# A transformer layer on one core: other buffers and another order in the opening, a division and a count moved

## The chip, the cores and the metric

The kernel runs on one core of one Trainium2 chip. The metric is the device time of one execution in microseconds; lower is better. Engines are called by their names and by their letters in the profile: TensorE (PE, and PEld for its weight loads), VectorE (DVE), ScalarE (ACT), GpSimd (POOL), SyncE (SP, which only issues DMAs).

## The reference

Eight sequences of 512 tokens with 256 channels go through attention, a layer norm, a mixture of experts with a shared expert, and a second layer norm. Cut to what matters:

```python
qkv = x @ w_qkv.T                       # 16 heads of 16 channels
q, k = rms_norm(q, q_norm_w), rms_norm(k, k_norm_w)
q, k = rope(q, k, cos, sin)             # q1*cos - q2*sin, q2*cos + q1*sin
attn = softmax(causal(q @ k.T) * scale)
x = layernorm(x + (attn @ v) @ w_proj.T)
normed = x * rsqrt(mean(x*x) + 1e-8) * norm_weight
shared = relu(normed @ sw1 + sb1) @ sw2 + sb2
probs = sigmoid(normed @ router_w.T); scores, idx = top_k(probs, 2)
routed = sum over the 2 chosen experts of weight * (relu(normed @ ew1 + eb1) @ ew2 + eb2)
x = layernorm(x + shared + routed)
```

## The kernel before

All matrix products run in fp16 on TensorE with each fp32 operand split in a high and a low half, so that one product is three (high by high, high by low, low by high).

**Steps.** The front (0 to 465 us) works on the eight batches (sequences) in an order written out by hand. Every engine runs through the same numbered steps, g from -40 to 209, and in each step does what is due in it, in the order in which its `step` function lists the kinds of work. An engine's queue is strictly in order. A table such as `QK = (-28, -24, -20, -16)` gives the step of each of the four token tiles, counted from 20 times the batch's number; for batches 0 and 1 the table `OPENING` gives other steps. Twenty units of scores (`UNITS`) of batch c stand in steps 20c to 20c + 19, so the steps below 0 are the opening, in which only batch 0 is prepared.

**What prepares a tile n (four a batch).** TensorE makes its q and k (`QK`) into a PSUM bank. ScalarE copies them (`copied`, L861) and squares them (L864). GpSimd multiplies the swapped halves by the sines (`swap`, two products, L667 and L670) into `rsum`. VectorE multiplies by the cosines (`rope`, L1111, into `rot`), sums the squares (L1118), and adds both (`summed`, L1126). For each pair of tiles ScalarE takes the inverse root (`roots`, step `ROOT`) and VectorE refines it in three small steps (`refined`, L1134 to L1136, step `REFINE`). VectorE scales (`normed`, L1141, step `QN`) into `qn`. GpSimd casts that to the high half (`nat_high`, L679), VectorE makes the low half (`nat_low`, L1151), and GpSimd doubles both for stacked contractions (`nat_twice`, L686 and L687). TensorE turns q and k (`stacked`, L1598 and L1604, step `TR`) through the banks `ma` and `mc`, and they are copied into `stk` by ScalarE (L950, L955) and VectorE (L1377). The unit 0 of a batch waits until all four tiles are in `stk`. The buffers `rsum`, `qn` and `nat` hold two tiles each. The bank `ma` is used in turn by the QK products from batch 1 on, the turned q and the V products, and each user waits for the copy of the one before it.

**Attention and after.** `scores` (L1553, L1562) fill two slots in turn; ScalarE takes the exp (`exps`, L847); `attended` multiplies by V (L1575). The rows are turned back (`NAT`, L1710) through the one bank `mb`; VectorE divides them by their sums (`averaged`, L1159 and L1160), which frees `mb` for the next tile. Then come the projection, the layer norm (GpSimd's `norms` and `shifted`), VectorE's normalised rows (`normalised`, L1200 to L1204), the turned normalised rows (`XN`, L1613, copied by ScalarE in L977), the router's product (`LG`, L1734), the choice of two experts (`chosen`, ending in the mask of L1224), the ranks (`RANK`), and GpSimd's scatter of the rows to the experts' regions (L717).

**The early tiles.** From step 161 on, the shared expert's first six tiles of 256 tokens run beside the last batches: H pieces are half of a hidden product (L1641, 24 matmuls), O pieces half of an output product (L1678). ScalarE takes the relu of an H piece (`early_hidden`, L902) and its high half (L906) one step later, and VectorE the low half (`early_low`, L1332) three steps later. Relus wait for the low half of the piece that used their buffer before.

**The tables.** In step `TABLE` (197) TensorE adds up how many rows each expert got (`counted`, L1622), once the last batch's ranks are summed; VectorE then works out the tables of tiles (`tables`), which the routed part (from 465 us on, L1786 and L1802) reads.

The changed functions are printed here with the line numbers of the profile.

Of the kernel before, what the change touches and what calls it, by code (L numbers as in the profile page):

```python
# [7 lines left out]
ALU = mybir.AluOpType  # L8
# [60 lines left out]
def wait_apart(eng, S, name, count):  # L69
# [10 lines left out]
MORE_WEIGHTS = -29  # L80
# [33 lines left out]
    QK: ((-40, -39, -38, -37), (0, 1, 3, 5)),  # L114
    ROPE: ((-40, -39, -36, -35), (1, 2, 4, 6)),
    ROOT: ((-38, -34), (2, 7)),
    REFINE: ((-37, -33), (4, 8)),
    QN: ((-37, -36, -33, -32), (4, 5, 8, 10)),
    V: ((-36, 2), (8, 22)),
    SPLIT_X: ((None,), (-31,)),  # L120
    TR: ((-28, -27, -26, -25), (9, 11, 14, 18)),
# [50 lines left out]
assert len(EARLY_AT) == 4 * N_EARLY and list(EARLY_AT) == sorted(EARLY_AT) and N_EARLY % 2 == 0  # L172

# [66 lines left out]
def program(nc, a, S, keep):  # L240
# [87 lines left out]
    with ExitStack() as ctx:  # L328
# [117 lines left out]
        with nc.Block() as block:  # L446
# [176 lines left out]
            def _(pool):  # L623
# [33 lines left out]
                def swap(n):  # L657
# [8 lines left out]
                    r1 = rsum[:, n % 2, :].rearrange("p (k h d) -> p k h d", k=2, d=HD)  # L666
# [7 lines left out]
                def nat_high(n):  # L674

                    pool.wait_ge(S("qn_done"), n + 1)
                    if n >= 2:
                        pool.wait_ge(S("tk_done"), n - 1)
# [3 lines left out]
                def nat_twice(n):  # L682

                    pool.wait_ge(S("nat_lo"), n + 1)
                    q, k = nat[:, n % 2, 0], nat[:, n % 2, 1]
# [126 lines left out]
            def _(act):  # L812
# [52 lines left out]

                def roots(c, u):
# [51 lines left out]
                def early_step(g):  # L918
# [6 lines left out]
                    for kind, m, q in early_due(g - 1):  # L925
# [15 lines left out]
                def step(g):  # L941
# [6 lines left out]
                    for c, t in due(TR, g):  # L948
# [4 lines left out]
                        if c == 0 and t < NT - 1:  # L953
# [104 lines left out]
            def _(dve):  # L1058
# [62 lines left out]
                def summed(c, t):  # L1121
# [4 lines left out]
                    then(dve.tensor_tensor(rsum[:, n % 2, :], rot[:], rsum[:, n % 2, :], ALU.add), "rsum_done", n + 1)  # L1126
# [11 lines left out]
                def normed(c, t):  # L1138
# [3 lines left out]
                                           rsum[:, n % 2, :].rearrange("p (h d) -> p h d", d=HD),  # L1142
# [3 lines left out]
                def nat_low(c, t):  # L1146
# [3 lines left out]
                    half = nat[:, n % 2].rearrange("p k h d -> p (k h) d")  # L1150
# [206 lines left out]
                def step(g):  # L1357
# [13 lines left out]
                    for c, t in due(TR, g):  # L1371
                        if c == 0 and t < NT - 1:
# [7 lines left out]
                    for c, t in due(NAT, g):  # L1380
                        averaged(c, t)
# [147 lines left out]
            def _(pe):  # L1529
# [62 lines left out]
                def stacked(c, t):  # L1592
# [4 lines left out]
                    for i in range(8):  # L1597
                        last = pe.transpose(ma[:, 64 * i:64 * i + 64].bitcast(F16),  # L1598
                                            nat[:, n % 2, 0, 2 * i:2 * i + 2, :].rearrange("p h d -> p (h d)"), ident_h[:])
# [324 lines left out]
```

## Time and profile before

| | |
|---|---|
| median of 3 runs | 982.53 us (982.53 to 987.88) |
| the profiled execution | 980.02 us, span 978.3 us |
| TensorE busy | 906.0 us (93%) |
| VectorE busy | 606.2 us (62%) |
| ScalarE busy | 626.0 us (64%) |
| GpSimd busy | 475.5 us (49%) |
| mean granted TensorE clock | 0.981 |

The span is the time from the first to the last instruction of the one execution that was profiled; all rows are from it. Busy times are summed over the instructions of an engine. Matmuls are pipelined and overlap a little in the records, so sums of their times are a few per cent high. The granted clock is 1.00 for TensorE's full 2.4 GHz and 0.50 for its half.

### The profile page before, as it was taken

The numbers are of one execution on the slowest core, as the hardware profiler recorded it, in microseconds if no ns is written. First come the engines' busy times: TensorE is split into PE (matmuls) and PEld (weight loads), VectorE is DVE, ScalarE is ACT, GpSimd is POOL, SyncE is SP. The second block draws the span as 40 slices with busy tenths as digits, with TensorE's granted clock in tenths as the row PEclk, the third lists the DMA queues.
The fourth block names the chain that finished last, engine by engine and source line by source line (L and its number), as shares of the span: only waits on it lengthen the run. The fifth ranks groups of instructions, "written<-read, shape, count | busy, mean of one in ns | idle before, by whom it ended". The sixth has DMA issues, their size and how long they took to land.

```text
span 978.3 us, 26286 instructions
## 1 busy us (share of the span) xinstructions
PE 906.0 (93%) x9049; PEld 694.1 (71%) x9050; DVE 606.2 (62%) x1197; ACT 626.0 (64%) x1027; POOL 475.5 (49%) x664
## 2 busy tenths in 40 slices
PE   3689899898999898989999999999999999999995
PEld 1344555454555546878989888998899988688885
DVE  7676799889898955875334444454433332327975
ACT  3688898787888776634655565556544544456753
POOL 5574566877777655474234454344434444312311
PEclk9699999999999999999999999999999999999998
DMA  5112223434323255587872121121212111139751
GB/s 171 66 66 91 93 98 105 136 108 154 110 88 115 104 171 184 192 287 260 283 249 65 49 70 57 63 65 54 70 50 65 55 61 62 46 102 287 224 162 44
DMA packets 69811, 116.98 MB, mean 120 GB/s; under 512 B 7808, under 2 KB 46080, under 8 KB 69600
## 3 DMA queue, kind: packets, MB, share of 16 engines
q1 hardware_dynamic: 52352, 81.51, 25.2%
q10 hardware_dynamic: 10896, 16.40, 5.8%
q0 software_dynamic: 6480, 17.97, 5.0%
q8 instruction: 51, 0.84, 0.3%
q14 instruction: 32, 0.26, 0.1%
HBM read 68.67 MB, written 47.18 MB: 118 GB/s over the span
## 4 chain that ended last, share of the span: by engine, by line
PE 65%; POOL 12%; DVE 9%; issue 6%; ACT 6%; DMA 1%; ACTq 0%; POOLq 0%; DVEq 0%; SPq 0%
PE yb L1802 25%; PE hb L1786 25%; PE pv_bank L1575 3%; PE yb L1678 2%; ACT prob L847 2%; POOL xg_rows L717 2%; PE hb L1641 2%; PE ma L1588 2%; POOL nat L679 2%; PE tr L1661 2%; POOL nat L686 1%; PE slot L1553 1%; POOL rsum L667 1%; POOL rsum L670 1%; POOL vv L696 1%
## 5 line engine op out<-in xcount | busy, mean ns | idle before, releaser
L1011 ACT ACTIVATE hf<-hb,b 128x256 f32<-128x256 f32 (+1 forms) x392 | 155.5, 454 | 212.8 <-PE hb L1786 193.8
L1786 PE MATMUL hb<-xgT,wts 128*128 128x256 f16 (+1 forms) x1872 | 219.0, 263 | 2.7 <-ACT hf L1011 2.7
L1802 PE MATMUL yb<-wts,hh 128*128 x1704 | 215.3, 273 | 0.0
L1430 DVE TENSOR_TENSOR hh<-hf,hh 128x1024 f16<-128x1024 f32 (+1 forms) x98 | 118.4, 1212 | 149.8 <-ACT hh L1016 149.8
L1786 PEld LDWEIGHTS hb<-xgT,wts 128*128 x1872 | 177.8, 98 | 25.4 <-issue 4.3
L782 POOL DMA_INDIRECT y_tok<-yb,dest x71 | 77.1, 1085 | 235.4 <-DVE yb L1442 225.2
L847 ACT ACTIVATE prob<-slot 128x1024 f32<-128x1024 f32 x160 | 162.3, 1044 | 32.4 <-PE slot L1562 32.1
L1802 PEld LDWEIGHTS yb<-wts,hh 128*128 128x128 f16 x1704 | 166.4, 98 | 21.2
L1016 ACT ACTIVATE hh<-hf 128x1024 f16<-128x1024 f32 (+1 forms) x98 | 97.6, 996 | 3.1
L717 POOL DMA_INDIRECT xg_rows<-xnh,sl_i x64 | 73.7, 1152 | 16.2 <-issue 13.9
L1442 DVE SCALAR_TENSOR_TENSOR yb<-yb,b2bc 128x512 f32<-128x512 f32 (+1 forms) x39 | 25.1, 643 | 86.7 <-PE yb L1802 81.6
L1553 PE MATMUL slot<-stk 64*128 64x128 f16 (+3 forms) x512 | 64.1, 309 | 15.5 <-ACT prob L847 8.9
L1575 PE MATMUL pv_bank<-prob,vst 128*32 128x512 f32 (+3 forms) x1024 | 75.5, 436 | 1.1 <-ACT prob L847 1.1
L1588 PE MATMUL ma<-wqkv,xTh 128*128 128x256 f16 (+1 forms) x360 | 67.6, 333 | 4.1 <-ACT raw L864 2.2
L1575 PEld LDWEIGHTS pv_bank<-prob,vst 128*32 128x32 f32 x1024 | 30.0, 109 | 44.9 <-issue 37.6
L1562 PE MATMUL slot<-mask_b,ident_b 128*128 128x256 bf16 (+1 forms) x320 | 57.2, 262 | 0.0
L1786 PE MATMUL hb<-xgT,wts_s 128*128 128x256 f16 x480 | 54.0, 273 | 0.0
L1802 PE MATMUL yb<-wts_s,hh 128*128 128x256 f16 x480 | 53.9, 273 | 0.0
L1588 PEld LDWEIGHTS ma<-wqkv,xTh 128*128 128x128 f16 x360 | 34.8, 102 | 24.2 <-issue 5.1
L1802 PEld LDWEIGHTS yb<-wts_s,hh 128*128 128x128 f16 x480 | 47.0, 98 | 5.4
L1786 PEld LDWEIGHTS hb<-xgT,wts_s 128*128 128x128 f16 x480 | 47.0, 98 | 5.4
L1553 PEld LDWEIGHTS slot<-stk 64*128 64x128 f16 x512 | 17.2, 94 | 45.6 <-issue 18.2
(217 smaller groups left out, 1483.2 us busy)
## 6 DMA issues: line engine op xcount, KB each, us to landing
wts<-in_w_all SPq DMA_DIRECT2D x19, 512.0 KB, 4.9
stage<-in_w_all SPq DMA_DIRECT2D x16, 512.0 KB, 4.5
w_split<-chunk_hl SPq DMA_DIRECT2D x16, 512.0 KB, 3.0
wts<-y_tok SPq DMA_DIRECT2D x32, 256.0 KB, 4.8
xg<-xg_rows ACTq DMA_DIRECT2D x30, 264.0 KB, 2.7
wts<-w_split SPq DMA_DIRECT2D x3, 2048.0 KB, 9.8
xTf<-in_xT SPq DMA_DIRECT2D x8, 512.0 KB, 4.1
xin<-in_x SPq DMA_DIRECT2D x8, 512.0 KB, 4.2
```

The costliest lines, as they stand in the source:

```text
L717: pool.indirect_dma_start(a["xg_rows"], bass.IndirectOffsetOnAxis(ap=sl_i[:, c % 2, t, k:k + 1], axis=0), xnh[:, c % 2, t, :], None).then_ ...
L782: pool.indirect_dma_start(a["y_tok"], bass.IndirectOffsetOnAxis(ap=dest[:, slot, j:j + 1], axis=0), yb[:, par, j, :], None).then_inc(S(f"y ...
L847: act.activation(dst, src, ACT.Exp, scale=ATT_SCALE).then_inc(S("exp_done"), 1)
L1011: act.activation(hf[:, c, 0:size], hb[c // 2][:, (c % 2) * TT:(c % 2) * TT + size], ACT.Relu, bias=bias, scale=1.0 / WS).then_inc(S("relu_ ...
L1016: act.activation(hh[:, par, 0, cs, 0:size], hf[:, cs, 0:size], ACT.Copy).then_inc(S("h_hi"), 1)
L1430: dve.tensor_tensor(hh[:, par, 1, cs, 0:size], hf[:, cs, 0:size], hh[:, par, 0, cs, 0:size], ALU.subtract).then_inc(S("h_lo"), 1)
L1553: pe.matmul(slot[:, 512 * x + col:512 * x + col + T - P * j], stk[rows, par, 1, pr, P * j:P * j + P], stk[rows, par, 0, pr, P * j:T], star ...
L1562: last = pe.matmul(out, ident_b[:], mask_b[:, 0:diag[0], :], start=False, stop=True, skip_group_check=True)
L1575: last = pe.matmul(pv_bank[32 * r:32 * r + 32, P * j:T], vst[:, c % 2, j, 4 * g + r, :], prob[:, g % 2, r, SEG[j]:SEG[j] + T - P * j], sta ...
L1588: last = pe.matmul(out, xTh[:, c % 2, x, k, P * t:P * t + P], wqkv[:, y, k, cols], start=(n == 0), stop=(n == len(pieces) - 1))
L1786: ins = pe.matmul(hb[hc // 2][:, (hc % 2) * TT:(hc % 2) * TT + size], weights(e, c, w, hc * P, P), xgT[:, par, x * DC + c, 0:size], start= ...
L1802: ins = pe.matmul(ybank[par][:, j * D:(j + 1) * D], hh[:, par, x, hc, P * j:P * j + P], weights(e, DC + hc * D // CH, w, hc * D % CH, D), ...
```

## The change

Four parts.

1. **The opening.** The high halves of batch 0's four tiles go from GpSimd to ScalarE (`first_high`). Tiles 2 and 3 of batch 0 get halves and sums of their own, in the part of `prob` that is not in use yet (`halves`, `rotated`), so that they wait neither for `qn` nor for the turned rows. Tile 0 is turned in step -33; the turned k of tiles 1 and 2 is now copied by VectorE, like that of tile 3 before. The next x^T is split, and the projection's weights too, some steps later.
2. **Batch 1's order.** Its first two QK products stand in steps -2 and -1, ahead of unit 0, and use the banks `mb` and `pv_bank`; their halves and turns come sooner; its V product goes from step 8 to 13.
3. **The first division sooner.** For tile 0 of every batch `averaged` moves from the head of step NAT to the tail of the step before it on VectorE, ahead of the normalised rows of the batch before.
4. **The end of the front.** ScalarE's relus of the piece ("H", 3, 1) come three steps later, in step 189, so that the last turned normalised rows (step 188) are copied ahead of them. TensorE's `counted` stands behind the early piece of its step instead of ahead of it.

The diff, cut to its core:

```diff
-MORE_WEIGHTS = -29
+MORE_WEIGHTS = -24
...
 OPENING = {
-    QK: ((-40, -39, -38, -37), (0, 1, 3, 5)),
-    ROPE: ((-40, -39, -36, -35), (1, 2, 4, 6)),
-    ROOT: ((-38, -34), (2, 7)),
-    REFINE: ((-37, -33), (4, 8)),
-    QN: ((-37, -36, -33, -32), (4, 5, 8, 10)),
-    V: ((-36, 2), (8, 22)),
-    SPLIT_X: ((None,), (-31,)),
-    TR: ((-28, -27, -26, -25), (9, 11, 14, 18)),
+    QK: ((-40, -39, -38, -37), (-2, -1, 3, 5)),
+    ROPE: ((-40, -39, -36, -35), (-1, 0, 4, 6)),
+    ROOT: ((-38, -34), (1, 7)),
+    REFINE: ((-37, -33), (2, 8)),
+    QN: ((-37, -36, -33, -32), (2, 4, 8, 10)),
+    V: ((-35, 2), (13, 22)),
+    SPLIT_X: ((None,), (-28,)),
+    TR: ((-33, -28, -27, -26), (7, 10, 14, 18)),
 }
...
+def early_relu_due(g):
+
+    return [piece for at, piece in EARLY if at + (4 if piece == ("H", 3, 1) else 1) == g]
...
-            return ma[:, 0:2 * D]
+            return (mb, pv_bank, ma, ma)[t][:, 0:2 * D] if c == 1 else ma[:, 0:2 * D]
+
+        def halves(n):
+
+            if n in (2, 3):
+                return prob[:, 1, n - 2, 0:1024].bitcast(F16).rearrange("p (k h d) -> p k h d", k=2, h=NH)
+            return nat[:, n % 2]
+
+        def rotated(n):
+
+            return prob[:, 1, n, 0:2 * D] if n in (2, 3) else rsum[:, n % 2, :]
...
                     pool.wait_ge(S("qk_copied"), n + 1)
-                    if n >= 2:
+                    if n >= NT:
                         pool.wait_ge(S("qn_done"), n - 1)
...
                     for c, t in due(QN, g - 1):
-                        nat_high(4 * c + t)
+                        if c >= 1:
+                            nat_high(4 * c + t)
...
+                def first_high(n):
+
+                    act.wait_ge(S("qn_done"), n + 1)
+                    act.activation(halves(n)[:, :, :, 0:HD].rearrange("p k h d -> p (k h) d"),
+                                   qn[:, n % 2, :].rearrange("p (h d) -> p h d", d=HD), ACT.Copy).then_inc(S("nat_hi"), 1)
...
-                    for kind, m, q in early_due(g - 1):
+                    for kind, m, q in early_relu_due(g):
                         if kind == "H":
                             early_hidden(m, q)
...
-                        if c == 0 and t < NT - 1:
+                        if c == 0 and t == 0:
                             act.wait_ge(S("tk_done"), t + 1)
                             act.activation(stk[:, 0, 1, :, t * P:(t + 1) * P],
...
+                    for c, t in due(QN, g - 1):
+                        if c == 0:
+                            first_high(t)
                     for c, u in due(ROOT, g):
                         roots(c, u)
...
                     for c, t in due(TR, g):
-                        if c == 0 and t < NT - 1:
+                        if c == 0 and t == 0:
                             continue
...
                     for c, t in due(NAT, g):
-                        averaged(c, t)
+                        if t > 0:
+                            averaged(c, t)
...
                     for c, t in due(ROPE, g):
                         rope(c, t)
+                    for c, t in due(NAT, g + 1):
+                        if t == 0:
+                            averaged(c, t)
                     for c, u in rows_due(g):
                         normalised(c, u)
...
                         if c >= 1:
                             pe.wait_ge(S("xT_lo"), c + NT)
-                            pe.wait_ge(S("ma_free"), NTH["qk", c, t])
+                            if c >= 2 or t >= 2:
+                                pe.wait_ge(S("ma_free"), NTH["qk", c, t])
...
-                    if g == TABLE:
-                        counted()
                     for kind, m, q in early_due(g):
...
                             if m == N_EARLY - 1 and q == 1:
                                 turn_rows(0, 1)
+                    if g == TABLE:
+                        counted()
```

## Rows read from the trace of the kernel before

**Rows 1.** Windows view: busy us of PE, PEld, DVE, ACT, POOL; then clock, DMA.
```profile
500.00:978.00 478.00, 465.51 (x4472) 413.21 (x4470) 229.10 (x352) 263.59 (x502) 170.49 (x245) 0.99 0.29 91
```

**Rows 2.** Chain of waits, 165 to 260 us, its share by line.
```profile
by line: issue 22.3%; POOL xg_rows L717 14.2%; POOL rsum L667 5.4%; POOL vv L696 5.4%; POOL nat L679 5.2%; POOL nat L686 4.9%; POOL rsum L670 4.2%; POOL vv L706 3.6%; POOL y L745 3.6%; POOL nat L687 2.9%; DVE nat L1151 2.1%; POOL vv L704 2.
```

**Rows 3.** GpSimd's timeline, opening: start, us, line, operation, idle before.
```profile
14.56 1.17 POOL L670 TENSOR_TENSOR rsum<-raw,stab 128x256 f32<-128x256 f32 x1
...
18.34 1.13 POOL L679 CAST nat<-qn 128x512 f16<-128x512 f32 x1 [2.62 <-DVE qn L1141]
...
30.61 0.61 POOL L679 CAST nat<-qn 128x512 f16<-128x512 f32 x1 [0.80 <-PE mc L1604]
...
34.28 1.07 POOL L687 COPY nat<-nat 128x512 f16<-128x512 f16 x1
```

**Rows 4.** VectorE's timeline, opening.
```profile
16.80 0.23 DVE L1134 TENSOR_TENSOR nt<-ry 128x64 f32<-128x64 f32 x1 [0.28 <-ACT ry L876]
...
17.58 1.42 DVE L1141 TENSOR_TENSOR qn<-rsum,rn 128x512 f32<-128x512 f32 x2
...
26.80 0.52 DVE L1135 SCALAR_TENSOR_TENSOR nt<-ms,nt 128x64 f32<-128x64 f32 x1
...
32.35 1.51 DVE L1410 TENSOR_TENSOR xTh<-xTf,xTh 128x1024 f16<-128x1024 f32 x1
```

**Rows 5.** ScalarE's timeline, 19 to 49 us.
```profile
19.25 0.60 ACT L966 ACTIVATE vst<-ma 128x512 f32<-128x512 f32 x1 [1.57 <-PE ma L1588]
...
39.15 1.02 ACT L847 ACTIVATE prob<-slot 128x1024 f32<-128x1024 f32 x1 [1.64 <-PE slot L1562]
...
48.61 1.02 ACT L847 ACTIVATE prob<-slot 128x1024 f32<-128x1024 f32 x1
```

**Rows 6.** TensorE's timeline, 38 to 62 us.
```profile
38.17 0.61 PE L1553 MATMUL slot<-stk 64*128 64x512 f16 x2 [0.88 <-DVE stk L1377]
...
38.90 2.77 PE L1588 MATMUL ma<-wqkv,xTh 128*128 128x512 f16 x6
...
48.85 1.46 PE L1588 MATMUL ma<-wqkv,xTh 128*128 128x512 f16 x6 [0.85 <-ACT vst L966]
...
61.60 0.61 PE L1598 MATMUL ma<-keep_ident,nat 128*128 128x128 f16 x8 [2.48 <-ACT vst L966]
```

**Rows 7.** Windows view as above, around unit 0 and after the count.
```profile
38.00:44.00 6.00, 5.64 (x20) 1.83 (x21) 1.31 (x3) 3.13 (x4) 1.62 (x2) 0.54 0.50 197
...
436.00:440.00 4.00, 4.00 (x25) 2.88 (x22) 3.54 (x23) 0.84 (x2) 2.44 (x3) 0.57 1.02 382
```

**Rows 8.** Who waited for whom on TensorE, 100 to 375 us.
```profile
PE mb L1710 <- DVE an L1160: 9.1, 5, 2.5
```

**Rows 9.** VectorE's timeline, one batch of the middle.
```profile
223.08 2.55 DVE L1200 SCALAR_TENSOR_TENSOR xnf<-y,vv,ffn_nw 128x256 f32<-128x256 f32 x2
```

**Rows 10.** TensorE's timeline, 430 to 448 us.
```profile
430.16 0.95 PE L1734 MATMUL mc<-wrout,xnT 128*128 128x8 f16 x32 [2.24 <-ACT xnT L977]
...
435.77 0.26 PE L1622 MATMUL mc<-keep_msum,ones_h 128*128 128x8 f16 x4 [1.83 <-DVE keep_msum L1243]
...
435.89 7.07 PE L1641 MATMUL hb<-xgT,wts_s 128*128 128x256 f16 x48
...
442.79 5.40 PE L1678 MATMUL yb<-wts_s,hh 128*128 128x256 f16 x48
```

**Rows 11.** ScalarE's timeline, 429 us.
```profile
429.10 1.01 ACT L977 ACTIVATE xnT<-mc 128x1024 f16<-128x1024 f16 x1
```

**Rows 12.** VectorE's timeline, 429 to 450 us.
```profile
429.22 2.23 DVE L1332 TENSOR_TENSOR hh<-hf,hh 128x1024 f16<-128x1024 f32 x1 [2.60 <-ACT hh L906]
...
433.07 0.19 DVE L1224 TENSOR_TENSOR mh<-oh 128x32 f16<-128x32 f32 x1
...
447.54 2.34 DVE L1332 TENSOR_TENSOR hh<-hf,hh 128x1024 f16<-128x1024 f32 x2
```

**Rows 13.** GpSimd's timeline, 429 us.
```profile
429.11 1.26 POOL L769 TENSOR_TENSOR rs<-rs,b2s 128x512 f32<-128x512 f32 x1 [0.39 <-DMA rs<-resid]
```

More of the change, by code:

```diff
@@ L662, in swap @@
                     pool.wait_ge(S("qk_copied"), n + 1)
-                    if n >= 2:
+                    if n >= NT:
                         pool.wait_ge(S("qn_done"), n - 1)
                     q4 = qk_copy(n).rearrange("p (k h d) -> p k h d", k=2, d=HD)
-                    r1 = rsum[:, n % 2, :].rearrange("p (k h d) -> p k h d", k=2, d=HD)
+                    r1 = rotated(n).rearrange("p (k h d) -> p k h d", k=2, d=HD)
                     pool.tensor_tensor(r1[:, :, :, 0:hd2], q4[:, :, :, hd2:HD],
@@ L676, in nat_high @@
                     pool.wait_ge(S("qn_done"), n + 1)
-                    if n >= 2:
-                        pool.wait_ge(S("tk_done"), n - 1)
+                    pool.wait_ge(S("tk_done"), n - 1)
                     pool.tensor_copy(nat[:, n % 2, :, :, 0:HD].rearrange("p k h d -> p (k h) d"),
@@ L684, in nat_twice @@
                     pool.wait_ge(S("nat_lo"), n + 1)
-                    q, k = nat[:, n % 2, 0], nat[:, n % 2, 1]
+                    q, k = halves(n)[:, 0], halves(n)[:, 1]
                     pool.tensor_copy(q[:, :, 2 * HD:4 * HD], q[:, :, 0:2 * HD]).then_inc(S("nat_ready"), 1)
@@ L1125, in summed @@
                     dve.wait_ge(S("swap_done"), 2 * (n + 1))
-                    then(dve.tensor_tensor(rsum[:, n % 2, :], rot[:], rsum[:, n % 2, :], ALU.add), "rsum_done", n + 1)
+                    then(dve.tensor_tensor(rotated(n), rot[:], rotated(n), ALU.add), "rsum_done", n + 1)
                 def refined(c, u):
@@ L1141, in normed @@
                     then(dve.tensor_tensor(qn[:, n % 2, :].rearrange("p (h d) -> p h d", d=HD),
-                                           rsum[:, n % 2, :].rearrange("p (h d) -> p h d", d=HD),
+                                           rotated(n).rearrange("p (h d) -> p h d", d=HD),
                                            rn[:, t, :].unsqueeze(2).broadcast_to([P, 2 * NH, HD]), ALU.mult),
@@ L1149, in nat_low @@
                     dve.wait_ge(S("nat_hi"), n + 1)
-                    half = nat[:, n % 2].rearrange("p k h d -> p (k h) d")
+                    half = halves(n).rearrange("p k h d -> p (k h) d")
                     then(dve.tensor_tensor(half[:, :, HD:2 * HD], qn[:, n % 2, :].rearrange("p (h d) -> p h d", d=HD),
@@ L1598, in stacked @@
                         last = pe.transpose(ma[:, 64 * i:64 * i + 64].bitcast(F16),
-                                            nat[:, n % 2, 0, 2 * i:2 * i + 2, :].rearrange("p h d -> p (h d)"), ident_h[:])
+                                            halves(n)[:, 0, 2 * i:2 * i + 2, :].rearrange("p h d -> p (h d)"), ident_h[:])
                     last.then_inc(S("tq_done"), 1)
@@ L1604, in stacked @@
                         last = pe.transpose(mc[:, 64 * i:64 * i + 64].bitcast(F16),
-                                            nat[:, n % 2, 1, 2 * i:2 * i + 2, :].rearrange("p h d -> p (h d)"), ident_h[:])
+                                            halves(n)[:, 1, 2 * i:2 * i + 2, :].rearrange("p h d -> p (h d)"), ident_h[:])
                     last.then_inc(S("tk_done"), 1)
```

## The prediction

> **What bounds the kernel now.** Read first how little of the time the change can touch: from the last early tile on, TensorE is busy 465.5 of 478 us at full clock [rows 1], so that part only moves to the left by what is saved ahead of it. The change lives in the front, 0 to 465 us, and there three regimes follow one another in the chain of waits. In the opening (11 to 38 us) the chain runs through GpSimd's and VectorE's small steps while TensorE mostly waits. From 45 to 120 us it runs through TensorE and ScalarE. From 120 to 325 us it hardly leaves GpSimd and VectorE: table scatters, swaps, norms, halves [rows 2]. The reader should see that a wait of TensorE removed in the third regime is not a gain by itself.
>
> **The opening's limit is a shared resource.** A GpSimd copy of 512 elements takes 0.61 us alone and 1.13 when VectorE is in a two-input step [rows 3]; a small two-input step of VectorE takes 0.23 alone and 0.52 behind GpSimd [rows 4]. Start and end times fit strict turns: each waits until the other's instruction has ended. I therefore count turns: 0.60 for a large two-input step of VectorE and for a GpSimd product, 0.53 for a GpSimd copy, 0.2 for a small step.
> The Trainium skill (SBUF — State Buffer, the shared port pair) states an exclusive lock between GpSimd and a VectorE instruction with two SBUF inputs, in which the loser fully blocks; by this rule the trace agrees. If instead they only slowed each other evenly, the same sum would come out, so it changes no term.
>
> **Part 1, opening.** Removed from GpSimd: four high halves, 4 x 0.53 = 2.1 us of turns, now on ScalarE at 0.60 each (the V copy of the same 512 fp32 elements [rows 5]), where it waits anyway. Moved behind the fourth pair of turned rows: the low half of the next x^T, 1.1 of its 1.51 us [rows 4], and the low parts of the projection weights, 0.7. Removed waits: swaps 2 and 3 no longer wait for a buffer, since halves and sums of tiles 2 and 3 have their own.
> Step by step: GpSimd's second swap ends at 15.73 [rows 3], as before. Swap 2 now starts at once and takes turns with the sum and the three refining steps, which before began at 16.80 and took 0.23 each with GpSimd silent [rows 4]. Swaps 2 and 3 are four turns of 0.60 from 15.7; the sum ends at 17.0, refining at 19.2 instead of 17.55. So the first part gets **1.6 us later**: qn 0 and 1 at 19.9 and 20.6 (before, 1.42 from 17.58 [rows 4]). Now it pays back: product, row sums and low half of tile 2 and 0 until 22.5; GpSimd doubles tile 0 at 24.8; sum, product, sums, low half of the others until 25.5; tile 1 doubled at 27.4; refining 27.9; qn 2 and 3 at 28.6 and 29.3; low halves 30.0 and 30.7 with no wait for GpSimd's half and none for the turned rows (before 0.80 [rows 3]); tiles 2 and 3 doubled at 31.8 and 32.9. Before, the last doubling ended at 35.35 [rows 3]: **2.4 us sooner**. The bounds: if every turn falls badly 34.3, if none does 31.4.
> Then TensorE. Turned tile 3: ScalarE's copy of tile 2 ends about 33.9, transposes to 35.8 at the low clock. The x^T half, queued on VectorE behind tile 2's copy, lands at 35.2 and is covered by them. Now both products of batch 1 stand **ahead of** unit 0: 35.9 to 38.5, and 41.0 if the clock stays low (the first took 2.77 [rows 6]), 40.6 or less if it rises. Unit 0 moves from 38.17 [rows 6] to 41.1, the first exp from 39.15 to about 42.0. But the products no longer stand between the units: from 42.0 the exps run nearly back to back, exp 3 starts at 46.2 (before 48.61 [rows 5]) and batch 1's third product at 46.3 instead of 48.85 [rows 6]. **Term 1: -2.6 us** (bounds -1.1 and -4.5: the bounds of the doubling, and a rise of the clock in the middle of the products, worth 0.9 at most here: 6 matmuls take 2.77 at 0.54 and 1.46 later [rows 6, 7]).
>
> **Part 2, batch 1's order.** The V product leaves step 8, where the turn behind it waited 2.48 us for its copy at the end of ScalarE's queue [rows 6]. Turns now stand at 7 and 10, V at 13 between a QK product (12) and a turn (14): two trips to ScalarE and back there, which I cost at 0.5 us for the copy and the square behind one exp, as after 48.85. ScalarE stayed busy through most of the 2.48, so not all of it is worth anything: **Term 2: -1.0** (0 to -2.0). The first products of batch 1 in mb and pv_bank free ma and cost nothing; their readers are done before pv is written.
>
> **Part 3, first division sooner.** In batches 2 to 5 TensorE stood five times, 9.1 us in all, until VectorE had divided tile 0 of the attended rows, which was queued behind the normalised rows [rows 8]; of these the two scalings alone take 2.55, since scatters hold them up [rows 9]. Now the division comes first. It adds a wait: normalised rows, and GpSimd's and TensorE's use of them four steps later, stand behind the transposes of the next step. In the batches with a backlog these are done already. What is late next: VectorE has the same list of work, so the second division comes when it came, and TensorE stops there, about 2.5 us further on. As the chain in this regime is GpSimd's and VectorE's [rows 2], little reaches the end. **Term 3: -1.0** (0 to -9.1).
>
> **Part 4, the count behind the product.** TensorE stood 1.83 us for the last batch's sums [rows 10], and so late that the 48 matmuls behind them took 7.07 against 5.40 at full clock [rows 10], with 0.57 granted [rows 7]. Now H40 goes at once. The rows' copy, at 429.10 behind four relus [rows 11], now goes ahead of them, which takes away the 2.24 at the router product [rows 10]. But this does not arrive. The choice of experts on VectorE stands behind the low half of H31. That now starts some 0.9 (the copy) after 429.22, but it ran 2.23 only because GpSimd held the turn to 430.37 [rows 12, 13]; it still ends at 431.4, so the mask is ready at 433.26 as before [rows 12]. The idle time merely moves ahead of the ranks: H40 starts at 433.7 instead of 435.89. **Term 4: -2.2.** Counting comes at 436.4, by when VectorE has made the tables' constants; the tables delay the low half of H40, which ended 448.7 [rows 12]; its user O40 comes at 449.5 without a stop. Bounds -1.2 (the stop is 1 us) and -2.2.
> **Term 5, clock there:** 7.07 - 5.40 = 1.67 if it does not fall, 0 if it does behind the new 2 us of idle time; I take **-0.7**.
>
> **Sum:** 2.6 + 1.0 + 1.0 + 2.2 + 0.7 = 7.5 us. The profiled execution took 980.02 (span 978.3), so 972.5 by it; the median of the runs, 982.53, is 2.5 above it, and the runs spread by 5.3. I forecast for the median: 982.5 - 7.5 = **975.0**.
>
> **Rivals.** (a) *TensorE's waits for the division are real time.* Then term 3 is -9.1 and the clock stays up in those batches: 975.0 - 8.1 = 966.9. For it: ScalarE idled behind these waits too. Against it: the chain. 0.15. (b) *Only the tail works.* Collisions of swaps and refining cost what the halves give, and the new wait for V at 13 replaces the old: terms 1 to 3 are 0, 982.5 - 2.9 = 979.6. 0.25. (c) *Slower: the softmax starts too late.* Unit 0 behind two products at the low clock; with the doubling at its upper bound the first exp starts at 43.4, 4.3 later than 39.15. If ScalarE's exps pace the next 80 us, the delay stays; less 2.2 of the tail and 0 elsewhere, 982.5 + 2.1 = 984.6. It decides when TensorE and ScalarE are without gaps between exp 0 and exp 3; before, exp 3 came 9.5 after exp 0 [rows 5], which four exps of 1.02 leave mostly open, so I give it 0.07. (d) *The count gives nothing*, since the early tiles wait for the tables instead: 975.0 + 2.9 = 977.9. 0.08. My forecast: 0.45.
>
> **How the numbers follow.** The forecast's own range by its bounds is 970 to 979. To hold 8 in 10 I take 967 to 981. About 1% (9.8 us) is what a measurement here tells from no change. Faster by more than that, under 972.7: all of (a) and a quarter of the forecast, 0.27. Slower by over 1%, above 992.4: no case reaches it, 0.02. Within: 0.71.
>
> **What would show it.** GpSimd's last doubling at 32.9 and no row of L679's kind before 40; refining near 18 to 19 with 0.5 each; exp 0 near 42 but exp 3 near 46; no 2.48 at the first turn of batch 1; in batches 2 to 5 a wait for the second division where there was one for the first, and VectorE's and GpSimd's chain as long as before; H40 about 6.8 us ahead of 435.9, with about 2 us of idle time ahead of the ranks. Wrong would make it: products at a low clock beyond 41, a QK product waiting for x^T, or batches of the middle whose length changes by more than 1 us.

## The result and the profile after

The changed kernel takes **977.73 us** (median of 9 runs, 974.94 to 982.55) against 984.62 for the kernel before beside it (9 runs, 982.53 to 990.1): ratio **0.9927, interval 0.9910 to 0.9945**, some 7.2 us faster. Measured again beside the last experiments it was 975.36 against 980.56, ratio 0.9948 (0.9934 to 0.9963), 5.2 us by the medians. The forecast was 7.5. The profiled execution took 976.9 us (span 975.2; before 980.02 and 978.3), with a mean clock of 0.981, as before. So the two profiles that are compared below differ by 3.1 us only, less than half of the timed gain: the execution of the kernel before that was profiled was faster than each of its nine timed runs.

From the last early tile on nothing changed but the place: 462.43 of 475 us busy at the same clock, as in [rows 1].

```profile
500.00:975.00 475.00, 462.43 (x4444) 410.40 (x4440) 228.03 (x351) 262.75 (x501) 168.80 (x245) 0.99 0.29 91
```

**The opening.** First VectorE's timeline, which answers to [rows 4], then GpSimd's, to [rows 3] (start, us, line, operation, idle before).

```profile
16.51 0.63 DVE L1158 TENSOR_TENSOR nt<-ry 128x64 f32<-128x64 f32 x1
```

```profile
31.33 0.61 POOL L701 COPY prob<-prob 128x512 f16<-128x512 f16 x1
```

The refining steps are nearly three times as long (0.63 to 0.65 against 0.23), since GpSimd's second pair of swaps now runs beside them. This repays itself: the last doubling ends at 31.94 instead of 35.35. TensorE's timeline answers to [rows 6].

```profile
34.78 2.23 PE L1616 MATMUL mb<-wqkv,xTh 128*128 128x512 f16 x6
36.85 1.46 PE L1616 MATMUL pv_bank<-wqkv,xTh 128*128 128x512 f16 x6
38.24 0.39 PE L1581 MATMUL slot<-stk 64*128 64x512 f16 x2
...
45.09 1.46 PE L1616 MATMUL ma<-wqkv,xTh 128*128 128x512 f16 x6 [1.95 <-ACT vst L990]
...
57.93 0.61 PE L1581 MATMUL slot<-stk 64*128 64x512 f16 x2 [2.99 <-ACT prob L862]
```

Both products stand ahead of unit 0, which starts where it started before (38.24 against 38.17). How long the first of them takes differs from one execution to the next, with the clock: 1.47 to 2.71 us in the five profiles with parts 1 and 2, and unit 0 starts at 37.18 to 39.02 in them. Batch 1's third product is 3.76 us sooner. But a new stop of 2.99 us stands at 57.93, and in the windows view the clock (the third figure from the end) is at its low level from 57 to 64 us, 0.53, where it was at the high one before. First the kernel before, then the changed one:

```profile
57.00:64.00 7.00, 4.52 (x50) 2.81 (x51) 6.79 (x10) 6.81 (x11) 5.65 (x6) 1.00 0.40 140
57.00:64.00 7.00, 6.07 (x42) 2.92 (x46) 4.19 (x7) 4.75 (x5) 3.70 (x4) 0.53 0.65 225
```

ScalarE's timeline shows what TensorE waits for. Between two exps stand the copy of the turned q of batch 1's first tile, three steps of the root and the high half of x^T, 2.7 us from the first to the next exp:

```profile
53.71 0.59 ACT L867 ACTIVATE raw<-pv_bank 128x512 f32<-128x512 f32 x1
54.19 1.03 ACT L971 ACTIVATE stk<-ma 128x1024 f16<-128x1024 f16 x1
55.09 0.36 ACT L892 ACTIVATE ms<-ssq,eps 128x64 f32<-128x64 f32 x1
...
55.93 1.04 ACT L1012 ACTIVATE xTh<-xTf 128x1024 f16<-128x1024 f32 x1
56.87 3.05 ACT L862 ACTIVATE prob<-slot 128x1024 f32<-128x1024 f32 x3
```

**The middle.** Who waited for whom on TensorE, 100 to 375 us; the first row answers to [rows 8].

```profile
PE mb L1739 <- DVE an L1184: 10.0, 6, 3.5
PE slot L1581 <- ACT prob L862: 6.4, 11, 1.2
```

The wait for the division has not become smaller, 10.0 us against 9.1 (9.7 to 10.2 in the five profiles with the division sooner and the rows in their old place, 9.0 to 11.9 in the five with neither moved); it is now the second division that TensorE waits for. Yet batches 2 to 5 are shorter, by 0.78, 0.62, 1.32 and 0.63 us, measured from one second division to the next.

**The end of the front.** TensorE's timeline answers to [rows 10].

```profile
425.67 0.94 PE L1763 MATMUL mc<-wrout,xnT 128*128 128x8 f16 x32
426.47 2.78 PE L1706 MATMUL yb<-wts_s,hh 128*128 128x256 f16 x24
431.24 0.19 PE L1770 MATMUL mc<-mh,tri_h 128*128 128x32 f16 x1 [1.99 <-DVE mh L1248]
...
431.46 4.45 PE L1669 MATMUL hb<-xgT,wts_s 128*128 128x256 f16 x24
...
435.84 2.78 PE L1669 MATMUL hb<-xgT,wts_s 128*128 128x256 f16 x24
```

The idle time ahead of the router's product is gone and stands, 1.99 us of it, ahead of the ranks. The first 24 matmuls of the early product run at the low clock (4.45 against the 2.78 of the next 24), as they did in the kernel before. VectorE's timeline says why the ranks are no sooner than the batch itself: the choice begins behind the early low half, 2.08 us sooner than before (431.37), which is all the lead that the front had at that place.

```profile
428.02 1.34 DVE L1356 TENSOR_TENSOR hh<-hf,hh 128x1024 f16<-128x1024 f32 x1 [3.49 <-ACT hh L927]
429.29 0.18 DVE L1234 TENSOR_SCALAR lg<-mc 128x32 f32<-128x32 f32 x1
```

### The profile page after: what moved, and what is told of

It reads as the page before. It is cut to its first block, busy times and chain, and to the rows that moved or that the text cites. A ratio compares the mean times of both kernels' runs of the same rounds, so it can differ in the third digit from the quotient of the medians.

```text
span 975.2 us, 26284 instructions
## 1 busy us (share of the span) xinstructions
PE 906.3 (93%) x9049; PEld 695.5 (71%) x9050; DVE 601.4 (62%) x1199; ACT 626.9 (64%) x1029; POOL 466.4 (48%) x660
## 4 chain that ended last, share of the span: by engine, by line
PE 66%; POOL 10%; DVE 9%; ACT 7%; issue 6%; DMA 0%; ACTq 0%; POOLq 0%; DVEq 0%; SPq 0%
PE hb L1815 25%; PE yb L1831 24%; PE pv_bank L1603 4%; PE yb L1706 3%; ACT prob L862 2%; PE hb L1669 2%; POOL xg_rows L731 2%; PE slot L1581 2%; PE tr L1689 2%; PE ma L1616 1%; PE slot L1590 1%; POOL nat L693 1%; POOL rsum L682 1%; POOL y L759 1%; POOL vv L710 1%
## 5 line engine op out<-in xcount | busy, mean ns | idle before, releaser
L731 POOL DMA_INDIRECT xg_rows<-xnh,sl_i x64 | 76.1, 1189 | 16.2 <-issue 13.9
L1616 PE MATMUL ma<-wqkv,xTh 128*128 128x256 f16 (+1 forms) x348 | 61.6, 321 | 5.1 <-ACT raw L879 2.1
L810 POOL TENSOR_TENSOR rstd_f<-var_eps,keep_mhalf 128x2 f32<-128x2 f32 x16 | 11.9, 743 | 77.0 <-DVE var_eps L1521 77.0
```

Of the source, the lines that this page charges most:

```text
L731: pool.indirect_dma_start(a["xg_rows"], bass.IndirectOffsetOnAxis(ap=sl_i[:, c % 2, t, k:k + 1], axis=0), xnh[:, c % 2, t, :], None).then_ ...
L1616: last = pe.matmul(out, xTh[:, c % 2, x, k, P * t:P * t + P], wqkv[:, y, k, cols], start=(n == 0), stop=(n == len(pieces) - 1))
```

## The experiments

Ratios are to the kernel before on the same chip, with a 95% interval. The first four kernels shared one set of runs of before (median 985.81 us), the next four another (981.66), the last four a third (980.56). A gain in us is the ratio's share of that median, where it doesn't say "by the medians"; the two ways differ by up to 0.7 us.

**Parts 1 and 2 alone.** The changed kernel with parts 3 and 4 undone (the edit is cut):

```diff
-    return [piece for at, piece in EARLY if at + (4 if piece == ("H", 3, 1) else 1) == g]
+    return [piece for at, piece in EARLY if at + 1 == g]
...
                     for c, t in due(NAT, g):
-                        if t > 0:
-                            averaged(c, t)
+                        averaged(c, t)
...
-                    for c, t in due(NAT, g + 1):
-                        if t == 0:
-                            averaged(c, t)
...
+                    if g == TABLE:
+                        counted()
                     for kind, m, q in early_due(g):
```

> Parts 1 and 2 alone (opening and batch 1's order); the first division and the end of the front are as in the kernel before. My theory: the third QK product of batch 1 starts 3 to 4 us before 48.85, as in the trace of the changed kernel (45.09), but the turn of batch 1's tile 0, now in step 7, gathers four other tasks of ScalarE between two exps, so some 3 us are given back by 60 us, and the whole is 0 to 3 us faster than before. Rival 1 (the prediction's sum, terms 1 and 2): 3.6 us faster, kept to the end. Rival 2 (only the tail works): no difference.

Measured: 983.0 us, ratio 0.9978 (0.9961 to 0.9995), 2.2 us. That is within the expected 0 to 3; the prediction's 3.6 for the two parts lies just inside the interval (0.5 to 3.8 us).

**Part 3 alone**, in the kernel before:

```diff
                     for c, t in due(NAT, g):
-                        averaged(c, t)
+                        if t > 0:
+                            averaged(c, t)
...
                         rope(c, t)
+                    for c, t in due(NAT, g + 1):
+                        if t == 0:
+                            averaged(c, t)
```

> Part 3 alone: the first division moved ahead of the normalised rows, all else as before. The prediction: 1.0 us faster, as TensorE's wait for the first division becomes one for the second. Rival (a): 8 to 9 us faster. Middle theory from the trace of the changed kernel, where each of batches 2 to 5 is shorter by 0.6 to 1.3 us: 3 to 4 us faster by the start of batch 5's divisions.

Measured: 981.71 us, ratio 0.9962 (0.9942 to 0.9981), 3.7 us, as the middle theory had it; neither the prediction's 1.0 nor rival (a)'s 8 to 9 lies in the interval (1.9 to 5.7 us).

**Part 4 alone**, in the kernel before:

```diff
+    return [piece for at, piece in EARLY if at + (4 if piece == ("H", 3, 1) else 1) == g]
...
-                    for kind, m, q in early_due(g - 1):
+                    for kind, m, q in early_relu_due(g):
...
-                    if g == TABLE:
-                        counted()
                     for kind, m, q in early_due(g):
...
+                    if g == TABLE:
+                        counted()
```

> Part 4 alone: relus of one piece behind the last turned rows' copy, count behind H40. The prediction: 2.2 us faster at H40 counted from the choice of experts, and the same 2.2 at the first routed tile. Rival from the trace of the changed kernel: 2.2 at H40, but only 1.0 at the first routed tile, as the clock was low under H40 and H50 stopped for a while.

Measured: 983.57 us, ratio 0.9982 (0.9967 to 0.9998), 1.8 us. The interval (0.2 to 3.3 us) holds the prediction's 2.2 and the rival's 1.0.

**Part 1 alone.** As parts 1 and 2 alone, with batch 1's order and banks put back:

```diff
-    QK: ((-40, -39, -38, -37), (-2, -1, 3, 5)),
+    QK: ((-40, -39, -38, -37), (0, 1, 3, 5)),
...
-    V: ((-35, 2), (13, 22)),
+    V: ((-35, 2), (8, 22)),
...
-    TR: ((-33, -28, -27, -26), (7, 10, 14, 18)),
+    TR: ((-33, -28, -27, -26), (9, 11, 14, 18)),
...
-            return (mb, pv_bank, ma, ma)[t][:, 0:2 * D] if c == 1 else ma[:, 0:2 * D]
+            return ma[:, 0:2 * D]
```

> Part 1 alone: halves on ScalarE and own buffers in the opening, batch 1's order as before, its products behind units 0 and 1 in bank ma. My theory: unit 0 of batch 0 starts about 3 us sooner than 38.17, all of that is kept to 60 us, and the kernel is 2 to 4 us faster than before and at least as fast as with both parts. Rival: batch 1's order is what pays, then this one is within 1 us of before.

Measured: 982.73 us, ratio 0.9973 (0.9956 to 0.9989), 2.7 us, within the expected 2 to 4.

**What the four tell.** 2.2 + 3.7 + 1.8 = 7.7 us for the parts against 7.2 for the whole: they add up, as far as intervals of 1.5 to 2 us to either side of each part can tell. Part 1 alone gives as much as parts 1 and 2. The division, timed so, gives two to nearly six times what I had given it. In the trace of part 1 alone TensorE's timeline shows unit 0 at 35.76, 2.4 us sooner than before, of the 3.5 by which the last doubling is sooner there (it ends at 31.84 instead of 35.35):

```profile
35.76 0.61 PE L1577 MATMUL slot<-stk 64*128 64x512 f16 x2 [0.88 <-DVE stk L1401]
...
58.60 0.61 PE L1622 MATMUL ma<-keep_ident,nat 128*128 128x128 f16 x8 [2.24 <-ACT vst L990]
```

The old stop at batch 1's first turn is there too (2.24; 2.48 in [rows 6]). So part 2 exchanged that stop for the one of 2.99, and put 3.5 us of products ahead of unit 0.

**Why the division pays.** The wait of TensorE does not shrink, so another theory was needed. The prediction held that scatters stretch the two scalings to 2.55 us. Here is the place in batch 4 of the kernel before, GpSimd's timeline and VectorE's, and then VectorE's second scaling by itself:

```profile
268.38 1.29 POOL L717 DMA_INDIRECT xg_rows<-xnh,sl_i  x1 [0.16 <-issue]
269.67 0.62 POOL L686 COPY nat<-nat 128x512 f16<-128x512 f16 x1
270.23 0.62 POOL L687 COPY nat<-nat 128x512 f16<-128x512 f16 x1
270.79 0.62 POOL L679 CAST nat<-qn 128x512 f16<-128x512 f32 x1
271.57 0.98 POOL L717 DMA_INDIRECT xg_rows<-xnh,sl_i  x1 [0.17 <-issue]
```

```profile
269.53 2.55 DVE L1200 SCALAR_TENSOR_TENSOR xnf<-y,vv,ffn_nw 128x256 f32<-128x256 f32 x2
272.12 0.66 DVE L1203 CAST xnh<-xnf 128x512 f16<-128x512 f32 x1
272.82 0.77 DVE L1204 TENSOR_TENSOR xnh<-xnf,xnh 128x512 f16<-128x512 f32 x1
273.62 0.26 DVE L1159 RECIPROCAL rcp<-mb 128x16 f32<-128x16 f32 x1
```

```profile
271.61 0.47 DVE L1200 SCALAR_TENSOR_TENSOR xnf<-y,vv,ffn_nw 128x256 f32<-128x256 f32 x1
```

From 269.67 to 271.41 GpSimd makes three copies, and the first scaling ends only behind the last of them; the second comes to its end 0.67 us behind it. One scatter stands ahead of the copies. The other begins at 271.57, and the second scaling, which runs beside it, takes 0.47 all the same. And a pair of scalings that has a scatter beside it for its first 0.4 us, and no copy, takes 0.88. At 166 us of the same profile, GpSimd's timeline and VectorE's:

```profile
165.35 1.23 POOL L717 DMA_INDIRECT xg_rows<-xnh,sl_i  x1 [0.30 <-POOL xnh L714]
```

```profile
166.18 0.88 DVE L1200 SCALAR_TENSOR_TENSOR xnf<-y,vv,ffn_nw 128x256 f32<-128x256 f32 x2
```

In the kernel with part 3 alone, the place in batch 4 looks like this:

```profile
268.12 0.62 POOL L686 COPY nat<-nat 128x512 f16<-128x512 f16 x1
268.68 0.62 POOL L687 COPY nat<-nat 128x512 f16<-128x512 f16 x1
269.23 0.62 POOL L679 CAST nat<-qn 128x512 f16<-128x512 f32 x1
```

```profile
267.98 0.26 DVE L1159 RECIPROCAL rcp<-mb 128x16 f32<-128x16 f32 x1
268.27 0.42 DVE L1160 TENSOR_TENSOR an<-mb,rcp 128x256 f32<-128x256 f32 x1
268.61 1.92 DVE L1200 SCALAR_TENSOR_TENSOR xnf<-y,vv,ffn_nw 128x256 f32<-128x256 f32 x2
```

The division (read from PSUM) runs at its normal 0.26 and 0.42 beside the first copy, and the scalings meet only two in full: 1.92 us. All four of these pairs, in batches 2 to 5, go from 2.55 or 2.56 to 1.92: 2.5 of the 3.3 us by which the four batches get shorter. The next kernels test that reading: they move the same rows out of the copies' way.

**The rows sooner, in the changed kernel.**

```diff
-XN_ROWS = (38, 43)
+XN_ROWS = (38, 41)
```

> The changed kernel, with the second pair of normalised rows of batches 0 to 5 in step 41 instead of 43 (the list XN_ROWS: 38, 41). My theory now: in batches 2 to 5 VectorE's list sets the pace, and the division sooner paid because the two scalings no longer ran into three GpSimd copies (2.55 us) but into two (1.92), not because TensorE waits less (10.0 us against 9.1). Two steps earlier VectorE stands idle for 1.78 us, waiting for GpSimd's high half, and the rows are ready; so some 2.0 us of work (0.88, 0.43, 0.69) goes into idle time and 3.3 us leave the crowded place. Each of batches 2 to 5 gets 1 to 2 us shorter: 4 to 8 us faster than the changed kernel, 11 to 15 faster than the kernel before (ratio near 0.987). Rival, TensorE's path sets the pace: the division comes no sooner, nothing gained, ratio 0.993. Second rival: the rows hold up GpSimd's high half two steps earlier by as much as they free later: 0 to 1 us, ratio 0.992 to 0.993.

Measured: 972.94 us, ratio 0.9914 (0.9901 to 0.9927), 8.4 us.

**The rows sooner, in the kernel before** (the same line, nothing else).

> The kernel before with that same move of the second pair of rows from step 43 to 41, and nothing else; the division stays where it was. If VectorE's list and the collision with GpSimd's copies are the cause, this takes 4.0 us (2.55, 0.66, 0.77) out of the place ahead of the division and puts 2.0 into idle time: each of batches 2 to 5 gets 1.6 to 2.5 us shorter, 6 to 10 us faster than the kernel before in all (ratio 0.990 to 0.994), and TensorE's waits for the first division shrink although the division did not move. If it was the division's own place that paid, the rows' place is worth less than the 3.7 us of the division alone: 0 to 3 us.

Measured: 976.45 us, ratio 0.9952 (0.9936 to 0.9967), 4.7 us. TensorE's waits for the division, 100 to 375 us, although the division was not moved (9.1 in [rows 8]):

```profile
PE mb L1710 <- DVE an L1160: 3.5, 4, 1.6
```

And VectorE's timeline of the changed kernel with the rows sooner, at the place where the changed kernel idles for 1.78 us:

```profile
260.94 1.09 DVE L1224 SCALAR_TENSOR_TENSOR xnf<-y,vv,ffn_nw 128x256 f32<-128x256 f32 x2
262.07 0.80 DVE L1227 CAST xnh<-xnf 128x512 f16<-128x512 f32 x1
262.90 1.09 DVE L1228 TENSOR_TENSOR xnh<-xnf,xnh 128x512 f16<-128x512 f32 x1
```

Both came out under my expectation (11 to 15 and 6 to 10), and the kernel before with the rows sooner above the 0 to 3 that was to hold if the division's own place had paid. So VectorE's list counts, but not all that leaves its crowded place arrives: the rows took 2.98 us where the idle time was 1.78. And the two moves don't add, as the table shows. It gives stretches of each profiled execution, in us. A batch's mark is the start of VectorE's reciprocal of its second tile. The first column is the time of batch 0's mark, the next two are distances between marks, and the last is from batch 7's mark to the first routed tile.

| kernel | batch 0 | batch 1 to 5 | 5 to 6 | 7 to routed |
|---|---|---|---|---|
| before | 96.10 | 184.76 | 34.24 | 71.96 |
| changed | 95.60 | 181.41 | 38.04 | 70.93 |
| changed, again | 96.62 | 181.53 | 37.00 | 69.65 |
| parts 1 and 2 | 96.03 | 184.78 | 37.46 | 71.94 |
| part 1 | 94.53 | 184.59 | 37.54 | 71.97 |
| part 3 | 96.98 | 181.42 | 38.05 | 74.52 |
| part 4 | 100.03 | 184.07 | 37.57 | 70.28 |
| changed, rows sooner | 95.20 | 179.94 | 35.09 | 69.66 |
| before, rows sooner | 96.42 | 180.13 | 35.09 | 73.63 |
| changed, turn later | 96.52 | 181.82 | 36.98 | 69.70 |
| without part 2 | 93.13 | 181.28 | 36.94 | 68.33 |
| without part 2, rows sooner | 94.42 | 180.13 | 35.10 | 69.74 |
| the same, no division | 93.08 | 180.26 | 35.10 | 69.66 |
| count only | 96.45 | 184.21 | 35.47 | 68.80 |

Second column: four batches take 184.1 to 184.8 with neither move, 181.3 to 181.8 with the division sooner, 179.9 to 180.3 with the rows sooner, with or without the division. Third column: with the division sooner (and the rows in their old place) TensorE waits longer once, in batch 5, and its clock is low behind that wait for longer (0.77 to 0.78 granted in the 15 us from batch 5's mark, in all five profiles with it, 0.91 to 1.00 in the five with neither move). These are TensorE's timeline and a window of the changed kernel, where the kernel before had a stop of 2.47 and a granted clock of 0.76 in 320 to 327 us:

```profile
320.62 1.08 PE L1739 MATMUL mb<-ident_f,raw 128*128 128x128 f32 x4 [3.50 <-DVE an L1184]
```

```profile
320.00:327.00 7.00, 6.38 (x46) 4.61 (x46) 4.87 (x13) 5.49 (x7) 4.59 (x5) 0.54 0.47 172
```

That gives back 2.5 us (a mean of 37.4 in five profiles, against 34.9 in the two without the move and without the stop told at the end). A low clock there does not need the longer wait: the count alone, with a stop of 2.37, had 0.53 in the same window, and took 1.2 us longer to the next mark than the kernel before. With the rows sooner the column is 35.1. The first column is the least certain: kernels with the opening of before give 96.10 to 96.98, and once (part 4 alone) 100.03. The last column is 71.9 to 74.5 in the five without part 4 or the count's move, and 68.3 to 70.9 in the nine with it.

**The turn of tile 0 later**, in the changed kernel:

```diff
-    TR: ((-33, -28, -27, -26), (7, 10, 14, 18)),
+    TR: ((-33, -28, -27, -26), (9, 10, 14, 18)),
```

> The changed kernel with tile 0 of batch 1 turned in step 9 instead of 7, as before the change. Theory, a pile-up on ScalarE: in step 7 the copy of the turned q (1.03), the roots and the half of x^T stand between two exps, TensorE waits 2.99 us at 57.93 and its clock falls to half for 7 us. Then this kernel has no such stop, no low clock near 57, and is 1 to 3 us faster than the changed one (ratio 0.990 to 0.992). Rival: ScalarE has the same work in the same stretch, the stop moves or the clock falls elsewhere: within 0.5 us of the changed kernel (ratio 0.9927).

Measured: 975.9 us, ratio 0.9941 (0.9928 to 0.9954), 5.8 us: between the 7.2 and the 5.2 of the changed kernel, so no gain. The stop is split, not gone, and the clock is low from 58 to 65.5 us as well:

```profile
57.21 0.39 PE L1581 MATMUL slot<-stk 64*128 64x512 f16 x2 [1.54 <-ACT prob L862]
...
59.13 1.01 PE L1626 MATMUL ma<-keep_ident,nat 128*128 128x128 f16 x8 [1.31 <-ACT stk L971]
```

The pile-up theory falls in so far as it blamed the turn's step; the rival, that ScalarE has this work in this stretch anyway, holds.

**Without part 2.** The changed kernel with the edit of "part 1 alone" to batch 1's order.

> The changed kernel with part 2 undone: batch 1's products, halves, turns and V product in the steps and banks of before; parts 1, 3 and 4 stay. Theory: parts add up and part 2 is worth nothing, since parts 1 and 2 together gave -2.2 and part 1 alone -2.7: this is within 0.7 us of the changed kernel, ratio 0.992 to 0.9935. Rival, part 2 pays once the division is sooner, by the 1.0 us that I had given it: ratio 0.9935 to 0.995.

Measured: 973.12 us, ratio 0.9917 (0.9901 to 0.9933), 8.5 us by the medians, a little better than the expected 0.992 to 0.9935. Its interval doesn't reach the rival's 0.9935.

**The changed kernel again**, no edit.

> The changed kernel itself, beside the others on one chip. The kernels before had gained 8.7 us (rows sooner), 8.5 (without part 2) and 5.8 (turn later) on the chip of the last comparison, on which the changed kernel did not run. Expected: 5.5 to 9 us faster than the kernel before, ratio 0.991 to 0.9945.

Measured: 975.36 us, ratio 0.9948 (0.9934 to 0.9963), 5.2 us by the medians, just under the expected 5.5.

**Without part 2 and the rows sooner** (both edits).

> The changed kernel without part 2 and with the second pair of rows in step 41. If the two effects add (part 2 costs some 1 us; the rows sooner give 1.5 to 4 more on VectorE's list), 10 to 13 us faster than the kernel before, ratio 0.987 to 0.990, and the fastest of all. Rival: both gains were one and the same, or differences of chips: it stands with the changed kernel, ratio 0.992.

Measured: 970.73 us, ratio 0.9897 (0.9881 to 0.9914), 9.8 us by the medians, at the edge of the expected 10 to 13. Beside the changed kernel on the same chip it is 4.6 us faster, and the intervals of the two don't meet.

**The same without the division's move.**

```diff
-                        if t > 0:
-                            averaged(c, t)
+                        averaged(c, t)
...
-                    for c, t in due(NAT, g + 1):
-                        if t == 0:
-                            averaged(c, t)
```

> The same with the division back at the head of its step: parts 1 and 4 and the rows in step 41. If the division's new place paid only by letting the scalings run into two of GpSimd's copies instead of three, nothing is left for it once the rows are out of the way: within 0.5 us of the kernel with it. If TensorE's wait for the division is worth something by itself, 1 to 3 us slower than the kernel with it.

Measured: 969.96 us, ratio 0.9890 (0.9873 to 0.9908), 10.6 us by the medians, the lowest of all medians, 0.8 us under the kernel with the move, from which its interval doesn't set it apart. Nothing is left for the division's place once the rows are out of the way, as the new theory said.

**The count alone**, in the kernel before: of part 4's edit only the move of `counted`.

> The kernel before with the count behind the early piece and nothing else; the relus stay where they were. My step said that copying the rows ahead of the relus gives nothing by itself: then this is as fast as the whole of part 4, which gave 1.8 us, ratio 0.998. Rival: the early product behind the late row copy gains only its own 1.8 us of idle time and loses it again to the low clock: 0 to 1 us, ratio 0.999 to 1.000. In the trace H40 then starts at 434.1 (435.89 less 1.83), against about 433.5 with the relus moved as well.

Measured: 977.66 us, ratio 0.9970 (0.9958 to 0.9982), 2.9 us: no less than the whole of part 4 (1.8, with an interval of 0.2 to 3.3). TensorE's timeline:

```profile
430.25 0.91 PE L1734 MATMUL mc<-wrout,xnT 128*128 128x8 f16 x30 [2.22 <-ACT xnT L977]
...
433.88 2.78 PE L1641 MATMUL hb<-xgT,wts_s 128*128 128x256 f16 x24
...
436.61 2.78 PE L1641 MATMUL hb<-xgT,wts_s 128*128 128x256 f16 x24
```

The 2.22 stay ahead of the router's product and none stand ahead of the ranks. From the choice to the early product 2.47 us pass, against 2.17 with the relus moved and 4.52 in the kernel before. Copying the rows ahead of the relus is worth 0.3 us there and nothing that can be timed. It has a price, too: it puts the idle time right ahead of the early product, whose first 24 matmuls took 4.12 to 4.45 us in seven of the eight profiles with all of part 4 (2.78 in the eighth, the one without part 2), and 2.78 here. From the choice to the first routed tile the kernel before takes 33.5 us, the count alone 30.4, and the eight 29.8 to 32.5, five of them 31.2.

## Why the prediction was right, and where not

The time and the side were right: 975.0 forecast; 977.7 beside a kernel before that itself stood 2.1 higher, so 7.2 (and 5.2) against 7.5. That the sum fits so well is in part luck: two terms were off, in opposite directions, and a third was right for another reason than the one that I gave. One sign of the prediction was not met: the early product H40 stands 4.4 us ahead of 435.9 (3.2 in the second profile of the changed kernel), not 6.8. And one came that was to make it wrong, stretches of the middle that change by more than 1 us: batch 4 by 1.32, and the one from batch 5 to 6 by 3.8.

**Part 1, opening (term 1, -2.6).** Right in size, but not by its own path: the term took 2.4 us from the doubling and left unit 0 later, and had the moved products of part 2 bring the gain. Part 1 alone, without them, measured 2.7 (1.1 to 4.3), with the doubling 3.5 sooner and unit 0 2.4 sooner. For terms 1 and 2 together, forecast 3.6, parts 1 and 2 gave 2.2. The turns were counted well where they crowd (refining 0.63 to 0.65) and too dearly in the second half: the last doubling ended at 31.94, not 32.9. That the shared turns are what sets these durations agrees with these rows. The step about the products was half wrong: they started at 34.78 and ran at 2.23 and 1.46, not from 35.9 and at 2.77 or little less, so unit 0 came at 38.24 and not at 41.1, and rival (c), a softmax that starts too late, never had its condition. The third product came 3.76 sooner, more than forecast, and by batch 0's second division 0.5 of it was left.

**Part 2, batch 1's order (term 2, -1.0).** Wrong. Parts 1 and 2 gave 2.2, part 1 alone 2.7, a difference that the runs can't tell from none; in no set of runs was the time longer without part 2. What speaks against it is the mark of batch 0: 93.1 to 94.5 in the four profiles with part 1 and without part 2, and 95.2 to 96.6 in the five with both. The step that failed is "the V product leaves step 8, where the turn behind it waited 2.48": the wait was priced, but not what came in its place. I looked for it at the new V product, at step 13; it came in step 7, where the sooner turn meets the roots and the half of x^T on ScalarE (2.99 us and a low clock). That the turn's step alone is not the cause the turn-later kernel shows; which of the other moves of part 2 is, stays open.

**Part 3, first division sooner (term 3, -1.0).** Timed alone it gave 3.7 (1.9 to 5.7), so by that measurement the term was mis-sized. The forecast that the second division would come "when it came" failed: it came 0.6 to 1.3 us sooner in each of four batches. "VectorE has the same list of work" was right, and the list was shorter all the same, because [rows 9] was read wrongly: GpSimd's copies hold the scalings up (2.16 us for the one that meets three of them), not its scatters (0.47 beside one), and a division that reads PSUM is not held up by the copies (0.26 and 0.42). What the prediction did say came: the wait went to the second division, in the same total, and rival (a) was wrong.

That the whole of the 3.7 is this is not shown: the profiles have 3.3 us gained up to batch 5 and 2.5 given back behind it. From batch 0's mark to batch 7's they have 294.5 to 295.9 us with the division sooner and 296.6 and 296.8 in the two with neither move and without the stop told at the end, so 1.4 us by the means; against all five with neither move it is 3.5. So how often that stop comes may be what lies between the forecast's 1.0 and the measured 3.7; this stays open. (With the rows sooner the same distance is 291.1 to 292.3, 4.9 by the means without the stop, beside 4.7 timed.) In the last set of runs the count alone gave 2.9 of the changed kernel's 5.2, which leaves 2.3 for parts 1 to 3. The profile of part 3 alone is no help: its span is 2.2 us longer than that of the kernel before, and its last stretch alone 2.6 us longer: there the early product begins 6.2 us behind the choice instead of 4.5.

**Part 4 (terms 4 and 5, -2.9).** Right within the intervals: the count alone measured 2.9 (1.8 to 4.1), all of part 4 1.8 (0.2 to 3.3). The rows' copy gives nothing, as forecast, and the idle time moved ahead of the ranks, 1.99 us as against the "about 2". Of the clock term (a middle between 0 and 1.67) both ends occurred, and in the changed kernel it was nothing: the clock was as low as before behind the idle time (4.45 for 24 matmuls) and was not with the count alone (2.78).

**The rivals.** (b), only the tail, is refuted by part 1 and part 3 alone; (d) by the count alone.

## What to carry to other kernels

When two engines share turns, look at which instructions of the other engine lie inside a stretched one, start by start, before you name the cause; then move the stretched work to where the first engine idles. Here one number in a list of steps did what a reordering was meant to do, and did it without the longer wait. A wait that moves without getting smaller can still come with a gain, and a gain at one mark (3.76 us in the opening) can be gone at the next, so time each part alone and read the distance between marks, batch by batch, in more than one execution.

## What the runs showed of the hardware, unexpected

In three of the fourteen profiles ScalarE and VectorE both stop at the same place of the program in batch 6 and go on together, though TensorE had finished what they need 2.1 and 3.3 us earlier. VectorE's and ScalarE's timelines of parts 1 and 2 alone:

```profile
361.45 0.26 DVE L1183 RECIPROCAL rcp<-mb 128x16 f32<-128x16 f32 x1 [7.28 <-remote]
```

```profile
361.51 1.02 ACT L862 ACTIVATE prob<-slot 128x1024 f32<-128x1024 f32 x1 [5.13 <-remote]
```

The same stop is at 364.9 in part 4 alone and 359.9 in part 1 alone. It explains 3.2 us of the third column there (37.5 against 34.2), and TensorE's clock falls behind it (0.53 to 0.76 over the next 7 to 8 us, against 1.00 in the kernel before). All three are kernels with the division and the rows in their old places; two others of that kind, the kernel before and the count alone, do not have it, and none of the nine with a move does. Should it be frequent in the runs that are only timed, it would be part of what the division's move gained. For that speaks that the medians of the kernel before moved from 985.81 beside part 3 alone to 980.56 and 981.66 in the later sets. How often it comes was not counted, and what the engines waited for the profile does not show.
